# A transformer's tensor-engine stream: projections at full width, sixteen value products in halves of 64 columns

## The reference

```python
def attn_layer(x, Wqkv, qs, ksc, Wo):
    q, k, v = jnp.split(x @ Wqkv, 3, -1)          # 16 heads of 64
    q = l2norm(q) * qs; k = l2norm(k) * ksc        # then a rotary turn of q and k
    out = local_attention(q, k, v)                 # windows of 32, each sees itself and the one before
    return out.reshape(b, n, INNER) @ Wo
...
for i in range(DEPTH):                             # 6
    x = attn_layer(shift_tokens(x), ...) + x
    x = ffn_layer(shift_tokens(x), ...) + x
```

## Time and profile before

| | |
|---|---|
| median of 3 runs | 1687.85 us (1687.73 to 1692.02) |
| the profiled execution's own time | 1687.07 us |
| its span, first to last instruction | 1685.0 us |
| setup part | to about 230 us |
| units | about 230 to 1670 us |
| PE busy in the span | 1621.3 us |
| mean granted TensorE clock | 0.992 |

### The profile page before, as it was taken

The page is one execution under the profiler, slowest core; times in us unless marked ns, Lnnn a source line. Parts: engine busy times, 40 slices in busy tenths (PEclk is TensorE's granted clock), DMA queues, the critical chain, the costliest instruction groups (busy, mean ns, idle before and its releaser), DMA issues.

```text
span 1685.0 us, 70654 instructions
## 1 busy us (share of the span) xinstructions
PE 1621.3 (96%) x29226; PEld 1413.8 (84%) x29226; DVE 1482.9 (88%) x2314; ACT 1327.3 (79%) x2789; POOL 1334.1 (79%) x1798
## 2 busy tenths in 40 slices
PE   7999869999999999999999999999999999999997
PEld 5777547888888888898888989898898988988886
DVE  6887749999999999899999999999999999999984
ACT  6888737878878787887878788787888878888874
POOL 7777558888888888888888888888888888888870
PEclk9999989999999999999999999999999999999999
DMA  4588507566865656857567665658566667656654
GB/s 125 177 285 319 206 15 160 119 151 139 232 153 123 154 123 150 231 130 160 118 157 202 160 145 134 148 127 242 125 151 140 138 152 211 151 128 144 142 130 111
DMA packets 101407, 265.78 MB, mean 158 GB/s; under 512 B 26720, under 2 KB 34912, under 8 KB 101088
## 3 DMA queue, kind: packets, MB, share of 16 engines
q1 hardware_dynamic: 101088, 261.26, 61.5%
HBM read 45.15 MB, written 27.26 MB: 43 GB/s over the span
## 4 chain that ended last, share of the span: by engine, by line
PE 74%; POOL 5%; issue 3%; ACT 2%; SPq 1%; DVE 1%; DMA 0%; POOLq 0%; ACTq 0%; DVEq 0%
PE ps L1902 15%; PE ps L1893 15%; PE ps L1961 9%; PE ps L1917 9%; PE ps L1939 7%; PE ps L1949 4%; PE ps L2031 3%; PE ps L2020 2%; PE ps L2018 2%; PE ps L2019 2%; PE ps L1931 2%; POOL rot L1339 2%; POOL rot L1397 1%; SPq L1255 1%; PE ps L1992 1%
## 5 line engine op out<-in xcount | busy, mean ns | idle before, releaser
L1339 POOL TENSOR_TENSOR rot<-rot 128x512 f32<-128x512 f32 x380 | 492.0, 1311 | 50.7 <-DVE rot L1474 50.6
L1474 DVE TENSOR_TENSOR rot<-ps,rope_l 128x1024 f32<-128x1024 f32 x380 | 463.1, 1220 | 29.4 <-ACT sq L1638 17.6
L1397 POOL TENSOR_TENSOR rot<-rot,rnorm 128x1024 f32<-128x1024 f32 x190 | 362.2, 1906 | 17.7 <-POOL rnorm L1367 0.4
L1902 PE MATMUL ps<-w_t,xs_hi 128*128 128x256 f32 x1476 | 303.4, 298 | 13.2 <-PEq L374 11.0
L1648 ACT ACTIVATE un<-ps 128x512 f32<-128x512 f32 x384 | 229.5, 598 | 99.3 <-PE ps L1902 49.4
L1893 PE MATMUL ps<-w_t,xs_hi 128*128 128x512 f32 x784 | 262.9, 416 | 1.8 <-DVE rot L1474 1.7
L1638 ACT ACTIVATE sq<-ps 128x512 f32<-128x512 f32 x380 | 227.6, 599 | 45.2 <-PE ps L1893 24.5
L1902 PEld LDWEIGHTS ps<-w_t,xs_hi 128*128 128x128 f32 x1476 | 224.9, 189 | 27.8 <-issue 20.3
L1460 DVE TENSOR_REDUCE ssum<-sq 128x16 f32<-128x1024 f32 x190 | 230.1, 1211 | 12.3 <-ACT sq L1638 12.3
L1917 PE MATMUL ps<-ident_s,rot 128*128 128x128 f32 x1536 | 233.2, 274 | 6.0 <-ACT kT L1664 4.1
L1917 PEld LDWEIGHTS ps<-ident_s,rot 128*128 128x128 f32 x1536 | 180.5, 140 | 38.2 <-issue 15.4
(11 more groups left out here) (158 smaller groups left out, 3533.1 us busy)
## 6 DMA issues: line engine op xcount, KB each, us to landing
vk<-un SPq DMA_DIRECT2D x1440, 128.0 KB
w_t<-weights_dram SPq DMA_DIRECT2D x48, 512.0 KB, 6.7
weights_dram<-rot SPq DMA_DIRECT2D x12, 1024.0 KB, 5.1
weights_dram<-sq SPq DMA_DIRECT2D x24, 512.0 KB, 3.6
raw<-wqk_dram SPq DMA_DIRECT2D x24, 256.0 KB, 4.5
wvt_s<-wvt_dram SPq DMA_DIRECT2D x12, 256.0 KB, 5.2
wo_s<-wo_dram SPq DMA_DIRECT2D x12, 256.0 KB, 5.5
w_s<-w_dram SPq DMA_DIRECT2D x6, 341.0 KB, 4.3
```

What stands on the lines that cost most here:

```text
L1339: last = G.tensor_tensor(cos[:, :, s, :], cos[:, :, s, :], sin[:, :, 1 - s, :], ALU.add)
L1397: G.tensor_tensor(v, v, rnorm[:, t, kind * H:(kind + 1) * H, None].broadcast_to([P, H, D]), ALU.mult).then_inc(nrm_g.sem, 1)
L1474: V.tensor_tensor(dst, src[:, None, :, :].broadcast_to([P, 2, H // 2, D]), tab[:, :, None, :].broadcast_to([P, 2, H // 2, D]), ALU.mult).t ...
L1902: last = M.matmul(bank[:, cols], v, w_t[:, j, w, cols], start=i == 0, stop=i == 2)
```

## The change

All sixteen projections are written whole: `IN_HALVES`, `whole_products` and the branches of `proj` for halves go. In `values` of tile 1 the pairs 1 to 4 (sixteen products) are written in halves of 64 columns, apart from one product in the first two units of a layer. The two halves of one product now stand behind each other, where before the four products' first halves stood ahead of the four second halves. In the setup part four more entries stand in `HEADS_IN_HALVES`. The number of PE instructions of a unit is the same, and so is the number for eight units, 9216 with the waits; their places within a unit are not.

```diff
-HALVES = (slice(0, 256), slice(256, 512))
-IN_HALVES = ((1, 7), (0, 7), (0, 0), (0, 1), (0, 2), (0, 3), (0, 4), (0, 5))
-VALUES_IN_HALVES = ((1, 1),)
-HEADS_IN_HALVES = ((1, 0), (1, 1), (2, 0), (2, 1), (3, 1))
+HALVES = (slice(0, C // 2), slice(C // 2, C))
+HEADS_IN_HALVES = ((1, 0), (1, 1), (2, 0), (2, 1), (3, 0), (3, 1), (4, 0), (4, 1), (5, 0))
...
-                def whole_products(n, t, j):
-
-                    if (t, j) not in IN_HALVES or (t, j) == (0, 0) and n % B == 0:
-                        return 3
-                    return 1 if (t, j) == (0, 0) and n % B == 2 else 0
-
...
-                    products = ((x_hi, 0), (x_hi, 1), (x_lo, 0))
-                    whole = whole_products(n, t, j)
-                    for i, (v, w) in enumerate(products[:whole]):
-                        last = M.matmul(bank, v, w_t[:, j, w, :], start=i == 0, stop=i == 2)
...
-                    elif whole == 0:
-                        for cols in HALVES:
-                            for i, (v, w) in enumerate(products):
-                                last = M.matmul(bank[:, cols], v, w_t[:, j, w, cols], start=i == 0, stop=i == 2)
+                    M.matmul(bank, x_hi, w_t[:, j, 0, :], start=True, stop=False)
+                    M.matmul(bank, x_hi, w_t[:, j, 1, :], start=False, stop=False)
+                    last = M.matmul(bank, x_lo, w_t[:, j, 0, :], start=False, stop=True)
...
+                def in_halves(n, t, a, k):
+
+                    return t == 1 and 1 <= a <= 4 and not ((a, k) == (4, 3) and n % B in (0, 1))
+
...
-                        for cols in (slice(0, C // 2), slice(C // 2, C)) if (t, a) in VALUES_IN_HALVES else (slice(0, C),):
-                            for k in range(4):
+                        for k in range(4):
+                            for cols in HALVES if in_halves(n, t, a, k) else (slice(0, C),):
                                 last = M.matmul(ps[32 * k:32 * k + 32, SO[t], cols], pT[:, a, 32 * k:32 * k + 32], vk[:, 4 * t + k, a, cols],
                                                 start=a == 0, stop=a == PAIRS - 1)
```

More of the change, by code:

```diff
@@ L1889, in proj @@
                     bank = ps[:, PJ + PJ_BANK[t][j], :]
-                    products = ((x_hi, 0), (x_hi, 1), (x_lo, 0))
-                    whole = whole_products(n, t, j)
-                    for i, (v, w) in enumerate(products[:whole]):
-                        last = M.matmul(bank, v, w_t[:, j, w, :], start=i == 0, stop=i == 2)
-                    if whole == 1:
-                        for i in (1, 2):
-                            v, w = products[i]
-                            for cols in HALVES:
-                                last = M.matmul(bank[:, cols], v, w_t[:, j, w, cols], start=False, stop=i == 2 and cols is HALVES[1])
-                    elif whole == 0:
-                        for cols in HALVES:
-                            for i, (v, w) in enumerate(products):
-                                last = M.matmul(bank[:, cols], v, w_t[:, j, w, cols], start=i == 0, stop=i == 2)
+                    M.matmul(bank, x_hi, w_t[:, j, 0, :], start=True, stop=False)
+                    M.matmul(bank, x_hi, w_t[:, j, 1, :], start=False, stop=False)
+                    last = M.matmul(bank, x_lo, w_t[:, j, 0, :], start=False, stop=True)
                     if j < QK_BANKS:
```

## The result

The changed kernel takes 1680.24 us (median of 4 runs, 1677.40 to 1680.97) against 1687.80 for the kernel before in the same comparison (1687.73 to 1692.02). By the medians that is 7.6 us, 0.45%, faster; the ratio, which goes by the means of the runs, is 0.9946 with a 95% interval of 0.9931 to 0.9960, 0.54%. The profiled execution took 1677.40 us with a span of 1675.6; it is the fastest of the four, so profile against profile the gain is 9.7 us. In this document "my count" is made from the starts of PE's matmuls and of the instruction packets in the trace, over all units; a stall counts from 0.11 us on.

The account below looks back on a forecast made before the run. PE's instruction stream was taken as the bound, with stalls at instruction block ends; -7.7 (stalls) - 2.3 (projections) + 0.7 (values) + 0.1 (setup) = -9.2 us gave 1678.7 us from 1687.85, own range 1674 to 1684, 8 in 10 within 1673 to 1688.

Parts of the forecast that it names:

- The stall is the instruction block: PE's issue idle in `feed_w1` comes from 256-instruction blocks; rival that it is not the block: 1686.3 us, chance 0.08.
- The place of the block ends: Blocks behind the scores reach farther, to `feed_w1`, next projection or transposes; stalls 13.8 to 6.1 us, so -7.7 us.
- Other blocks ... both stay above 3.33.: Blocks from `values(before, 1)` into scores (3.75 us) and from `feed_w2` into `values` (4.2 us) would not stall.
- The fixed 3.3 us itself: A new block is ready about 3.3 us after the one before was begun; PE waits where 256 instructions take less.
- Projections whole: Eight projections of a unit with three matmuls of 512 columns instead of six of 256: -2.3 us.
- Values in halves: 24 more matmul pairs per unit in `values(before, 1)`: +0.7 us, between 0 and 1.4.
- I price the order at nothing: In `values`, four matmuls in a row on one column group cost nothing, since PE can reach 13 matmuls ahead.
- The slower rival: Halves in `values` cost as much as wholes, fewer column groups working at once: 1693 to 1722 us, chance 0.10.
- The floor of 25 ns: Least time for matmuls of 1 to 64 columns; by it the split values cost 0.55 us a unit, +26 us.
- The setup: 32 more matmuls in the setup part: 0 to 0.3 us, taken as +0.1 us.
- The sum: -7.7 - 2.3 + 0.7 + 0.1 = -9.2 us, giving 1678.7 us from the median.
- The gain given back: A rival: an engine close behind PE takes over, or blocks near 3.7 us stall instead; 1684 us, chance 0.10.

Follow-up runs that it names:

- short loads: Each load of values brings one of eight pairs of heads: 1677.32 us on the changed kernel, 1678.22 us on it with 32 fewer setup instructions.
- turn_plus16: groups_in_turn with one more head projection of the setup in halves, 16 more instructions: 1706.6 us, ratio 1.0102.
- groups_in_turn: Changed kernel with the split value products in the old order, first halves of all column groups ahead of the second halves: 1680.76 us, ratio 0.9944.
- before_minus16: Kernel before with one entry fewer in HEADS_IN_HALVES, 16 fewer setup instructions: 1672.2 us, ratio 0.9909.
- before_minus32: Kernel before with two entries fewer in HEADS_IN_HALVES, 32 fewer setup instructions: 1675.0 us, ratio 0.9906.
- before_minus48: Kernel before with three entries fewer in HEADS_IN_HALVES, 48 fewer setup instructions: 1687.47 us, ratio 0.9994.
- setup_minus32: Changed kernel with seven instead of nine entries in HEADS_IN_HALVES, 32 fewer setup instructions: 1693.37 us, ratio 1.0020.
- turn_minus16: groups_in_turn with one head projection of the setup fewer in halves, 16 fewer instructions: 1674.8 us, ratio 0.9923.
- whole_alone: Changed kernel with whole projections kept but values as in the kernel before, 1104 instead of 1152 instructions a unit: 1712.13 us, ratio 1.0134.

## Why the prediction was right

**The stall is the instruction block.** Right. The seven kernels in which only setup entries differ from a sibling have the same units, and their idle time moves from line to line and from 2.5 to 76 us in all. The Trainium skill, page "Runtime: NRT & Kernel Launch", section "Instruction fetch mechanics", says that crossing a block is mostly hidden. In the kernel before that holds for eight of the nine crossings in two units; the ninth cost 0.6 us and up to 5.5 us in the kernel with 96 instructions fewer, so the measurement decides. (By my count some of the eight cost a little too, 0.9 us in all.)

**The place of the block ends.** Right: five of the 23 places lie in `feed_w1`, six in the next projection and twelve in the transposes, as predicted; of the twelve two show a stall at all. Only one of the six is idle time in the waits of PE, where the prediction had some five; the others are delays of 0.1 to 0.2 us between starts. The sizes were 2.4, 1.2 and 0.4 us against 3.4, 2.1 and 0.6: 4.0 instead of 6.1.

**"Other blocks ... both stay above 3.33."** This step failed. The block that runs from `values(before, 1)` into the scores stalled at eight places, and one other block there once, for 2.7 us in all. With short loads these stalls are gone: value data are in flight there, and its packet starts 1.1 us behind the begin by the median, 0.9 with short loads. A time to readiness taken at a place with an empty DMA was used for one with a share of 0.96.

**The fixed 3.3 us itself** held at the one place from which it was read, and the change let the block there reach only a few instructions farther. In the runs with 32 and 96 fewer instructions and in turn_plus16 it gave forecasts that were wrong by 19 to 40 us. The prediction was right because it asked for the rule only next to where it was measured.

**Projections whole.** Sized too low: 0.096 us a unit, not 0.048. The earlier trace rows compare a halved with two whole projections that stand between other neighbours. With the same neighbours the gain is 2 to 24 ns, by what stands ahead.

**Values in halves.** The mis-sized term: +4.0 us against +0.7. The step that failed is "I price the order at nothing". Eight matmuls that start together showed that PE can look far ahead, not that it keeps four column groups busy when each gets four matmuls in a row; groups_in_turn put 0.071 of the 0.086 us on that. The slower rival had the right mechanism, at under a third of its smallest price of 0.3 us a unit. The floor of 25 ns by the page "TensorE: Matmul & The Clock Gate" of the Trainium skill, section "Back-to-back issue gap", gave an estimate of +26 us; measured were 0.086 us for 24 more matmuls, 3.6 ns each, and 0.6 ns with the groups in turn.

**The setup.** Not foreseen: 3.9 us, some 1.3 of it a wait on `u_raw` at 181.38 us that is not there after, the rest in the stretch where the clock was granted at half for a longer time before. It does not belong to the whole projections: the kernel before with 16 instructions fewer starts its first `scores` at 241.3 us, with 48 fewer at 242.4 and with 32 fewer at 244.1, those with whole projections between 241.4 and 243.8 us. So it goes with the place of the block ends or of the clock's steps in the setup, and no run tells these apart.

**The sum** was 0.5 us off in the profile (-9.2 against -9.7) and 1.5 us by the medians, but out of terms that missed by 2 to 4 us with both signs. The mechanism of the largest term was right; that the sum came so close was luck. Two slips in it change nothing here: its bounds at their best give 1675 and not 1674, and its chances for "within" add up to 0.19, not 0.15.

**The gain given back.** In small part this rival came too, where it was not looked for: ACT's waits did not grow, but PE now comes to the new weights of a layer before they have landed, +1.5 us.

What the change as a whole is, the last table says. Span less my count of stalls:

| kernel | median us | span | stalls | span less stalls |
|---|---|---|---|---|
| before | 1687.8 | 1685.0 | 14.6 | 1670.4 |
| before_minus16 | 1672.2 | 1669.8 | 2.5 | 1667.3 |
| before_minus32 | 1675.0 | 1673.5 | 3.9 | 1669.6 |
| before_minus48 | 1687.5 | 1682.4 | 14.8 | 1667.6 |
| changed | 1680.2 | 1675.6 | 6.7 | 1668.9 |
| setup_minus32 | 1693.4 | 1689.8 | 23.9 | 1665.9 |
| groups_in_turn | 1680.8 | 1677.7 | 10.5 | 1667.2 |
| turn_minus16 | 1674.8 | 1672.0 | 3.4 | 1668.6 |
| turn_plus16 | 1706.6 | 1706.3 | 42.3 | 1664.0 |

The last column differs by 3 us among the kernels with the units of before, and by 5 among the others; the stalls differ by 40. The count itself is good to a few us where stalls are many: taken only at every 256th instruction it is 12.8, 20.1 and 38.0 us in before_minus48, setup_minus32 and turn_plus16. The change is in effect a shift of the block ends: what it saves in the projections it spends in the values, and one setup entry taken from the kernel before gains twice as much by the medians (15.7 against 7.6 us; by the ratios 0.91 against 0.54%).

## What to carry to other kernels

Where PE is the bound and idles with the releaser "issue" at the same line again and again (here in every second unit), count instructions from stall to stall: if the distance is a multiple of 256, move the block ends with a few instructions in the setup before changing any of the work, and try several places, for one step of 16 moved this kernel by up to 26 us. A change to the number of instructions in a repeated unit is a change of all these places too, so it has to be compared at its own best place and not at the one that it happens to get. When matmuls are split, keep the halves of neighbouring column groups in turn. An "issue" wait that is not a multiple of 256 from the others can be a wait for data: here 14 of 194 were waits at new weights.

## What was unexpected of the hardware

- The packet of a block started between 1.4 us ahead of and 7.8 us behind the begin of the block ahead of it (both in `whole_alone`); it mostly took 0.9 to 1.6 us, and behind a stall PE went on 1.2 to 1.7 us after its end.
- Behind stalls of some 4.6 us in the scores the clock was granted at 1.2 GHz for up to 6.8 us.
- With nothing at all in flight a packet still started 3.8 us late, and in `feed_var` and around it the packet kept to a piece of work, not to the begin of its block.
- 24 more matmul pairs of 64 columns cost 15 ns with the column groups in turn and 86 ns with four matmuls in a row on each group.
- A projection of six matmuls of 256 columns is 2 to 24 ns longer than one of three of 512, by what stands ahead of it.
